# Three moves at the ends of an FFN, attention and FFN kernel's stages, and a redistribution of its opening over ScalarE, POOL and VectorE

## The reference

```
x = x + 0.5 * ffn(layernorm(x))
x = x + attn(layernorm(x))
x = x + 0.5 * ffn(layernorm(x))

ffn(x):  scores = sigmoid(x @ gate_w.T); idx = top_k(scores + gate_b, 4)
         w = 2.5 * scores[idx] / sum(scores[idx]); comb = w scattered over 16 experts
         y = sum_e comb[:, e] * ((silu(x @ gate_e.T) * (x @ up_e.T)) @ w2_e.T)
         y = y + (silu(x @ gate_s.T) * (x @ up_s.T)) @ w2_s.T
attn(x): q, k, v = x @ w_q.T, x @ w_k.T, x @ w_v.T; q, k rotated
         softmax(causal(q @ k.T / sqrt(128))) @ v, for each of 8 batches of 1024 rows
```

## Time and profile before

| | us |
|---|---|
| median of 3 runs | 815.38 (814.73 to 815.74) |
| the profiled execution | 816.33 |
| its span, first to last instruction | 814.5 |
| PE busy | 802.5 |
| DVE busy | 722.9 |
| POOL busy | 615.2 |
| ACT busy | 600.1 |

### The profile page before, as it was taken

One profiled execution on the slowest core, in us unless ns is written; L12 is line 12 of the kernel. 1 busy time (PEld: TensorE's weight loads), 2 busy tenths in 40 slices (PEclk: granted clock), 3 DMA queues, 4 the chain that ended last, 5 costly groups with the idle time before them and its releaser, 6 DMA issues. The chain is left out here.

```text
span 814.5 us, 15848 instructions
## 1 busy us (share of the span) xinstructions
PE 802.5 (99%) x4066; PEld 657.1 (81%) x4066; DVE 722.9 (89%) x2027; ACT 600.1 (74%) x1495; POOL 615.2 (76%) x560
## 2 busy tenths in 40 slices
PE   8999999999999999999999999999999999999998
PEld 7677777777778767899999998777777777777887
DVE  6899999999999988788888888789999999999986
ACT  5777788888786677776676766778788778886664
POOL 6777777777777679888888884477777777777764
PEclk9999999999999999999999999999999999999999
DMA  7567788878877746643333450556676776666653
GB/s 231 137 175 210 211 246 237 243 233 243 219 207 209 206 123 163 159 140 83 100 96 112 145 150 20 159 148 188 183 201 194 195 202 197 179 177 173 184 143 94
DMA packets 93480, 140.83 MB, mean 173 GB/s; under 512 B 10352, under 2 KB 39648, under 8 KB 93408
## 3 DMA queue, kind: packets, MB, share of 16 engines
q1 hardware_dynamic: 93408, 140.03, 61.6%
HBM read 112.67 MB, written 18.93 MB: 162 GB/s over the span
## 5 line engine op out<-in xcount | busy, mean ns | idle before, releaser
L633 POOL TENSOR_TENSOR h_l<-probT,h_h 128x512 fp32r<-128x512 f32 x254 | 330.0, 1302 | 137.4 <-ACT h_h L857 135.1
L857 ACT ACTIVATE h_h<-probT 128x512 fp32r<-128x512 f32 (+1 forms) x285 | 179.4, 629 | 58.2 <-DVE probT L1326 28.6
L1798 PE MATMUL bank<-xh,w_h 128*128 128x512 f32 x545 | 218.7, 401 | 2.4 <-DVE prob L1316 1.4
L1798 PE MATMUL bank<-xh,w_l 128*128 128x512 f32 x545 | 214.2, 393 | 0.0
L1798 PE MATMUL bank<-xl,w_h 128*128 128x512 f32 x545 | 213.8, 392 | 0.0
L920 ACT ACTIVATE bank<-bank 128x512 f32<-128x512 f32 x252 | 146.2, 580 | 68.5 <-PE bank L1798 65.9
L1326 DVE TENSOR_TENSOR probT<-prob,bank 128x512 f32<-128x512 f32 x255 | 172.6, 677 | 15.3 <-POOL h_l L633 3.6
L1316 DVE TENSOR_TENSOR prob<-bank,qkT 128x512 f32<-128x512 f32 x252 | 171.3, 680 | 15.6 <-ACT bank L920 11.2
L1798 PEld LDWEIGHTS bank<-xh,w_h 128*128 128x128 f32 x545 | 102.3, 188 | 40.5 <-DVE probT L1329 7.2
L1798 PEld LDWEIGHTS bank<-xh,w_l 128*128 128x128 f32 x545 | 102.3, 188 | 23.3
L1798 PEld LDWEIGHTS bank<-xl,w_h 128*128 128x128 f32 x545 | 102.3, 188 | 21.2
(11 more groups left out here) (143 smaller groups left out, 1340.5 us busy)
## 6 DMA issues: line engine op xcount, KB each, us to landing
qkT<-comb_rows SPq DMA_DIRECT2D x190, 256.0 KB, 5.2
qkT<-comb_rows SPq DMA_DIRECT2D x124, 128.0 KB, 3.0
rows<-comb_rows SPq DMA_DIRECT2D x28, 512.0 KB, 7.1
stage<-stage SPq DMA_DIRECT2D x64, 128.0 KB, 3.0
X<-in_x SPq DMA_DIRECT2D x16, 256.0 KB, 3.1
stage<-in_x_t SPq DMA_DIRECT2D x16, 256.0 KB, 6.7
x_t<-stage SPq DMA_DIRECT2D x16, 256.0 KB, 4.5
X<-x_rows SPq DMA_DIRECT2D x64, 64.0 KB, 5.8
```

Source lines behind the costliest of these rows:

```text
L633: nc.gpsimd.tensor_tensor(lo, f, hi.bitcast(F32), ALU.subtract).then_inc(done, 1)
L857: return nc.scalar.activation(dst, src, ACT.Copy)
L1798: return nc.tensor.matmul(dst, lhsT, rhs, start=start, stop=stop)
```

## The change

The parts of the diff, in the order of the program:

- **Opening, row sums.** Tile 3's means and variances were DVE's (`ffn_stats` and `ffn_mv` inside tile 0). Now ACT does them (`ffn_means`, `ffn_vars`, four instructions with an accumulator each), into a tensor of their own, `mv_3`.
- **Opening, scale of tile 2.** It was DVE's `ffn_scale` into PSUM. Now POOL does it in place (`first_scale`, after its low half of unit 4), so `ffn_xh` and `ffn_xl` of tile 2 read `xc` in SBUF. Two waits keep the buffers safe: PE's `ffn_logitsT` on `combT_done`, POOL's `ffn_center` on `xl_done`.
- **Opening, routing of tile 1.** `ffn_weighted` of unit 4 goes ahead of `ffn_take`, and `ffn_combT` ahead of unit 5's weighting.
- **End of the first feed-forward.** In tile 14 POOL's `attn_shift(0)` comes one unit earlier (after unit 1), and ACT's eight `attn_xn` start one unit earlier.
- **Attention.** At i = 0 of batches 1 to 6, DVE's `attn_scale(b + 1, 0)` stands behind `attn_residual` instead of ahead of it.
- **Start of the second feed-forward.** DVE's statistics of tile 19 go from inside tile 16 to ahead of the last `attn_residual`.

```diff
+            def first_scale():
+                pool.wait_ge(xc_done, 1)
+                nc.gpsimd.tensor_tensor(xc, xc, rows[:, 1, :], ALU.mult).then_inc(xs_done, 1)
...
-                    if j == 2 and first_batch == 0:
+                    if j == 1 and first_batch == 0:
                         attn_shift(0, rstd, neg_shift)
...
+                    if j == 4 and isinstance(T, int) and T == 0:
+                        first_scale()
...
-                copy(xh[q][:], bank[:, T_BANK, :]).then_inc(xh_done, 1)
+                copy(xh[q][:], xc if isinstance(T, int) and T == 2 else bank[:, T_BANK, :]).then_inc(xh_done, 1)
...
-                    at = j - (UNITS - 1 - NB)
+                    at = j - (UNITS - 2 - NB)
                     if 0 <= at < NB and first_batch == 0:
                         attn_xn(0, 2 * at)
                         attn_xn(0, 2 * at + 1)
...
                     copy(w2_h[:], w2_f).then_inc(w2_hi, 1)
+                    act.wait_ge(x_loaded[3], 16)
+                    ffn_means(3, 3, 1, 0, base)
+                    ffn_means(3, 3, 1, 1, base)
                     comb_spread(2)
                     opening_xh(1, 1)
                     ffn_silu(base, 0, 3)
                     ffn_h_hi(base, 0, 0)
                     comb_spread(3)
+                    ffn_vars(3, 3, 1, 0, base)
+                    ffn_vars(3, 3, 1, 1, base)
...
+                xs = xc if isinstance(T, int) and T == 2 else bank[:, m, :]
-                nc.vector.tensor_tensor(xl[q][:], bank[:, m, :], xh[q][:].bitcast(F32),
+                nc.vector.tensor_tensor(xl[q][:], xs, xh[q][:].bitcast(F32),
...
                     ffn_xl(N, 1 - q)
-                    dve.wait_ge(x_loaded[3], 16)
-                    ffn_stats(L, Lx, 1 - q)
                     ffn_weighted(T, q, 2)
-                    ffn_stats_wait(L)
-                    dve.wait_ge(var_done, 1)
-                    dve.wait_ge(neg_mean_done, 1)
-                    ffn_mv(L, 1 - q)
                     ffn_h(T, q, 2)
...
+                    ffn_weighted(T, q, 4)
                     ffn_take(N)
                     ffn_taken(N)
-                    ffn_weighted(T, q, 4)
                     ffn_mark(N)
                     ffn_h(T, q, 4)
                     ffn_weights(N)
+                    ffn_combT(N, 1 - q, True, base)
                     for j in range(5, PAIRS):
                         ffn_weighted(T, q, j)
-                        if j == 5:
-                            ffn_combT(N, 1 - q, True, base)
                         ffn_h(T, q, j)
-                    ffn_scale(T + 2, base)
                     ffn_h(T, q, PAIRS)
                     ffn_xl(T + 2, q)
...
                         attn_item(("v", 3), 0, 0, True)
-                    elif not last and i == 0:
-                        attn_scale(b + 1, 0)
                     if i >= 1:
                         attn_residual(b, p, i - 1)
                     elif not first:
                         attn_residual(b - 1, 1 - p, QB - 1)
+                    if not first and not last and i == 0:
+                        attn_scale(b + 1, 0)
...
             attn_scale(B, 1)
+            ffn_stats(TILES + 3, 3, 1)
             ffn_xl(TILES + 1, 1)
+            ffn_stats_wait(TILES + 3, TILES)
+            ffn_mv(TILES + 3, 1)
             attn_residual(B - 1, 1, QB - 1)
             ffn(TILES)
...
                 pe.wait_ge(xl_done, T + 1)
+                wait(pe, combT_done, T)
```

More of the change, by code:

```diff
@@ L137, in macaron @@
         mv = sb("mv", [P, QB, 2])
+        mv_3 = sb("mv_3", [P, NB, 2])
         var_eps = sb("var_eps", [P, QB])
@@ L408, in stats_count, with tile_mv @@
         def stats_count(T, base):
-            return T - (13 if base else -1)
+            return T - (14 if base else -1)
         def means_count(T, base):
-            return T - (7 if base else 3)
+            return T - (6 if base else 2)
+        def tile_mv(T, base):
+            if isinstance(T, int) and T == 3 and not base:
+                return mv_3[:]
+            return mv[:, NB * (T % 2):NB * (T % 2 + 1)]
         block = ctx.enter_context(nc.Block())
@@ L633, in low_half, with ffn_var @@
                 nc.gpsimd.tensor_tensor(lo, f, hi.bitcast(F32), ALU.subtract).then_inc(done, 1)
-            def ffn_var(T, at, base):
+            def ffn_var(T, at, base, src):
                 pool.wait_ge(mv_done, ln_count(T, base))
-                nc.gpsimd.tensor_tensor(var_eps[:, at], mv[:, at, 1], eps[:, at], ALU.add).then_inc(var_done, 1)
+                nc.gpsimd.tensor_tensor(var_eps[:, at], src[:, :, 1], eps[:, at], ALU.add).then_inc(var_done, 1)
             def ffn_rstd(T, base=0):
                 at = slice(NB * (T % 2), NB * (T % 2 + 1))
-                ffn_var(T, at, base)
+                ffn_var(T, at, base, mv[:, at])
                 nc.gpsimd.tensor_tensor(neg_mean[:, at], mv[:, at, 0], neg_one[:, at], ALU.mult).then_inc(neg_mean_done, 1)
@@ L661, in ffn_rows @@
                 at = slice(NB * q, NB * (q + 1))
-                ffn_var(T, at, base)
+                src = mv_3[:] if isinstance(T, int) and T == 3 else mv[:, at]
+                ffn_var(T, at, base, src)
                 wait(pool, combT_done, T - 2)
-                scale = root_d[:] if not isinstance(T, int) or T - base >= TURN_AHEAD else neg_one[:, at]
-                nc.gpsimd.tensor_tensor(comb[:, :, NEXP], mv[:, at, 0], scale, ALU.mult).then_inc(neg_mean_done, 1)
+                scale = root_d[:] if not isinstance(T, int) or T == 3 or T - base >= TURN_AHEAD else neg_one[:, at]
+                nc.gpsimd.tensor_tensor(comb[:, :, NEXP], src[:, :, 0], scale, ALU.mult).then_inc(neg_mean_done, 1)
                 pool.wait_ge(var_done, pool_count(T, base))
@@ L679, in ffn_center @@
                 wait(pool, xs_done, n - 1)
+                pool.wait_ge(xl_done, T)
                 nc.gpsimd.tensor_tensor(xc, xT[c], rows[:, 0, :], ALU.add).then_inc(xc_done, 1)
+            def first_scale():
+                pool.wait_ge(xc_done, 1)
+                nc.gpsimd.tensor_tensor(xc, xc, rows[:, 1, :], ALU.mult).then_inc(xs_done, 1)
             def ffn_tile(base, turn, c, first_batch=None):
@@ L884, in ffn_means @@
                     x = row_block(Tx, n) if base else raw_block(Tx, n)
-                    ins = nc.scalar.activation(unused[:, n, :, :], x, ACT.Identity, scale=MEAN_SCALE, accum_out=mv[:, NB * q + n, 0:1])
+                    ins = nc.scalar.activation(unused[:, n, :, :], x, ACT.Identity, scale=MEAN_SCALE, accum_out=tile_mv(T, base)[:, n, 0:1])
                 if part:
@@ L893, in ffn_vars @@
                     x = row_block(Tx, n) if base else raw_block(Tx, n)
-                    ins = nc.scalar.activation(unused[:, n, :, :], x, ACT.Square, bias=mv[:, NB * q + n, 0:1], scale=DEV_SCALE,
-                                               accum_out=mv[:, NB * q + n, 1:2])
+                    ins = nc.scalar.activation(unused[:, n, :, :], x, ACT.Square, bias=tile_mv(T, base)[:, n, 0:1], scale=DEV_SCALE,
+                                               accum_out=tile_mv(T, base)[:, n, 1:2])
                 if part:
@@ L1474, in ffn_tile @@
                 late = 1 if first else 0
-                if first:
-                    ffn_stats(L, Lx, 1 - q)
-                    ffn_stats_wait(L, base)
                 for j in range(PAIRS):
@@ L1482, in ffn_tile @@
                         attn_ln(0, 2)
-                    elif j == 0 and first:
-                        ffn_mv(L, 1 - q)
                     if step == 1:
```

## The result

| | before, us | after, us |
|---|---|---|
| median | 815.38 (814.73 to 815.74) | 827.13 (826.59 to 828.22) |
| the profiled execution | 816.33 | 826.59 |
| its span | 814.5 | 824.8 |

The changed kernel is slower: ratio 1.0148, 95% interval 1.0132 to 1.0164, or 11.75 us between the medians. The forecast was 823.9 us, with its own range of 822.8 to 825.0 and a wide one of 819.5 to 829.5. The sign and the main term are right. The time lies 3.2 us above the forecast, outside its own range, and near rival 1's 828.2.

A forecast was written before the change was run, and what follows sets the result against it. PE, busy 99% of the span, was taken as the bound. 816.33 + 8.5 + 0.3 - 0.3 = 824.8, less 0.95 for the median, gave 823.9 us; own range 822.8 to 825.0, wide range 819.5 to 829.5.

The forecast's parts named there:

- rival 1: Attention, batches 1 to 6: POOL's power instruction holds DVE's scale to its end, 12.8 us instead of 8.5, so 828.2; chance 0.35.
- Attention, +8.5 us forecast: Six batches: the scale behind the residual delays ACT's probabilities copy and PE's block 0 product by 1.42 us each.
- Rivals 2 and 3: Attention: half the stall given back, 819.7 us, chance 0.1; or copy not queued behind the split, 814.9 to 815.4, chance 0.06.
- rival 3: Attention batch starts: probabilities' copy not queued behind ACT's split, six batches cost 0 or gain 0.08 each; chance 0.06.
- Opening, +0.3 us forecast: Up to tile 2's router matmul: DVE's low half of tile 2 ends later, behind POOL's of unit 7; ends -0.6 and +0.6.
- two shifts of 0.3: Opening: fourth weighting 0.3 us earlier, transpose ahead of unit 5's weighting costs 0.30; taken to cancel.
- Tile 14, -0.3 us forecast: End of first feed-forward: earlier shift removes PE's 0.6 us wait for normalized rows, half lost again; ends -0.6 and +0.4.
- Second feed-forward and waits, 0 forecast: Start of second feed-forward: statistics move into idle time, 0, ends -0.2 and +0.2; extra PE and POOL waits met early, 0.

## Why the prediction was right, and where it was not

**Attention, +8.5 us forecast.** Right in mechanism and size. PE's six waits sum to 8.5 us; the attention took 8.17 more in the profiled executions, 7.8 by the experiment that takes it away, 9.3 (7.3 to 11.3) by the one that puts it in alone. The scale, at 352.27, came right behind the residual, and ACT's wait for it was 2.02 against 2.0 forecast.

**Rival 1, POOL's power instruction holds the scale** (the prediction's paragraph on the port pair calls it the second). Refuted: 0.69 us in all six batches, each time wholly inside that instruction. The Trainium skill, SBUF — State Buffer, section "SBUF: two separate sides", says that the shared port pair is an exclusive lock for the whole instruction, whoever starts first. By that, the scale would have ended behind 353.41, not at 352.96. The measurement decides: the profile's 1.65 us of that instruction on 8 columns do not hold DVE. That the final time lies near rival 1's 828.2 is a coincidence; its cause is another.

**Rivals 2 and 3.** No part of the stall was given back that a run could tell, and the copy stayed behind the split. Putting it ahead did not help either: rival 3's condition, "the copy not queued behind the split", was too weak. It would also have needed the exponentials free of the split.

**Opening, +0.3 us forecast.** From tile 1's router matmul to tile 2's the changed kernel took 16.34 us instead of 15.80 (all five traces with this opening: 16.33 or 16.34). That is +0.54, inside the forecast's ends; the matmul itself was 0.67 late, with the 0.13 that were there before. The step was right about the cause: POOL's low half of unit 6 kept to 1.30 us, and DVE's low half of tile 2 became the late one. ACT's four variances put one of its high halves 1.64 us later (22.51 instead of 20.87), and PE's second product with w2 began at 24.86 instead of 24.77: covered, as costed. PE's wait for the low half was 1.22 instead of 0.94, near the 1 foretold. The two rows that show it are DVE's low half, then POOL's of unit 7:

```profile
36.98 1.77 DVE L1218 TENSOR_TENSOR xl<-xn,xh 128x512 fp32r<-128x512 f32 x1
```

```profile
36.59 1.61 POOL L640 TENSOR_TENSOR h_l<-probT,h_h 128x512 fp32r<-128x512 f32 x1 [0.25 <-ACT h_h L873]
```

The low half ended at 38.75, 0.55 us behind POOL's 38.20, where I had reckoned 0.56. But POOL's instruction took 1.61 instead of 1.28, and this end, 0.27 us later than reckoned, is what the reckoning lacked. What lengthened it is not shown. All five traces with this opening have 1.61 to 1.64 at this place, but the other 27 of POOL's 128x512 instructions in this trace inside which such a DVE instruction starts took 1.29 to 1.31. The gate of unit 5 also had a wait of 0.82 us, where I had let two shifts of 0.3 cancel:

```profile
31.77 0.50 PE L1810 MATMUL bank<-xh,w_h 128*128 128x512 f32 x1 [0.82 <-DVE prob L1338]
```

PE came to it 0.21 sooner than before, as unit 4's weighting did come sooner, and unit 5's came 0.34 later. Over the whole kernel neither shows: 1.0004.

**Tile 14, -0.3 us forecast.** The transposes of the rows came 14.20 us after tile 15's router matmul, 0.37 sooner. The three traces with this edit and the fast pace have 14.30 or 14.31 there, and the five without it 14.55 to 14.58: 0.25 by the edit. ACT's first pair ran at 289.20, 2.1 us sooner by the same measure than in the earlier trace rows:

```profile
289.20 0.88 ACT L971 ACTIVATE xn<-X,neg_shift,rstd 128x128 f32<-128x128 f32 x2 [1.69 <-POOL neg_shift L779]
```

Right. The smaller wait foretold just ahead is there as well, in pieces too small for the list of waits:

```profile
291.91 0.40 PE L1810 MATMUL bank<-xh,w_l 128*128 128x512 f32 x1
292.28 0.49 PE L1810 MATMUL bank<-xh,w_h 128*128 128x512 f32 x1
```

That is 0.37 us from start to start, where 0.23 is the rule; the starts at 289.73 and 291.34 came 0.30 and 0.31 behind the ones before them.

**Second feed-forward and waits, 0 forecast.** Nothing is against it: the new waits alone gave 1.0013 (0.9996 to 1.003).

**What failed: a term that the sum did not have.** The prediction counted instructions and waits, and took each matmul at its old pace. The new array of 32 bytes was never a term.

Three pairs of kernels differ in the displacement alone. By their ratios it cost 3.6 us in the changed kernel (1.0148 and 1.0104), 3.9 with the attention order restored (1.0052 and 1.0004), and 1.7 in the kernel before (0.3 to 3.0). The tile periods make it 3 us, and with that the forecast of 823.9 would have been 826.9, beside 827.13 measured. The pace is shown, the size only to a microsecond or so. That the changed kernel without the displacement comes to just 823.9 is partly luck, since its interval reaches from 821.5 to 826.2.

Which of the arrays from `var_eps` to `h_l` it is, and why 32 bytes cost more than 64 or 128, stays open. The starts of PE's matmuls between 40 and 290 us narrow it: with 32 bytes the time from one 128x512 start to the next grew by 0.006 us behind `xh` times `w_h` and by 0.004 behind `xh` times `w_l`, and by -0.002 to +0.003 behind the other four, in all four traces with this displacement. No run moved `xh` alone, or kept the other engines from the arrays beside it.

## What to carry to other kernels

An instruction put behind one that waits for PE inherits that wait, and so does everything that its consumer has queued: look at the queue of the engine that reads the result before calling a swap of two neighbours free. When PE is 99% busy, a change to the list of on-chip arrays is an edit of its own: allocate new small arrays behind the operands of the matmuls, and compare the period of an undisturbed tile, which shows half a per cent (18.37 and 18.47 us) where no wait does. And compare stretches of a trace, not times since its start: two executions can be half a microsecond apart before the edit begins.

## What the runs showed of the hardware

- The pace of 128x512 matmuls in fp32r depended on where the on-chip arrays lie: 0.2301 us with the layout of before, 0.2329 with 32 bytes of displacement, 0.2319 with 64 and 0.2320 with 128, at a granted clock of 1.00 throughout.
- POOL's power instruction on 128x8 lasts 1.65 us and held a DVE instruction with two on-chip inputs not at all (0.69 us, six times), while a 128x512 one of POOL let such an instruction end only 0.55 to 0.56 us behind its own end.
